# A four-layer graph network: stores of x and of the turned rows moved between node phases, a bias moved behind the shares, one phase fused, and gathers released by counts

## What is computed

```python
h = jnp.maximum(_layernorm(x, axis=-1), 0.0)
x = x + _L0_gnn_ref(h, ...)   # attention with one head: out = segment_sum(h[src] * alpha) + bias
h = jnp.maximum(_layernorm(x, axis=-1), 0.0)
x = x + _L1_gnn_ref(h, ...)   # four heads, softmax over all edges, then:
#   heads = agg + x[None]; hn = layernorm(heads) * gamma + beta; hs = hn * sigmoid(hn)
#   (hs + (x @ Wr.T + br)) @ Wo.T + bo
h = jnp.maximum(_layernorm(x, axis=-1), 0.0)
x = x + _L2_gnn_ref(h, edge_attr_128, ...)   # filters from edge features, then an MLP on the sum
h = jnp.maximum(_layernorm(x, axis=-1), 0.0)
x = x + _L3_gnn_ref(h, ...)   # h + segment_sum(h[src]), then relu(@ W1 + b1) @ W2 + b2
```

## Time and profile before

| | |
|---|---|
| time, three runs | 4364.09 us median (4363.95 to 4365.29) |
| the profiled execution | 4362.5 us, span 4360.7 us |
| PE busy | 3646.0 us (84%) |
| POOL busy | 2881.8 us (66%) |
| DVE busy | 2136.9 us (49%) |
| ACT busy | 1362.1 us (31%) |
| DMA | 364.29 MB, mean 84 GB/s |

### The profile page before, as it was taken

How to read it: one execution, slowest core, us unless ns; L and a number is a source line. 1 busy time by engine, 2 the same in 40 slices (tenths; PEclk the granted TensorE clock), 3 DMA queues, 4 the chain that set the end, 5 groups by cost and what they waited for, 6 DMA issues and landing times. The chain is left out here.

```text
span 4360.7 us, 76651 instructions
## 1 busy us (share of the span) xinstructions
PE 3646.0 (84%) x20596; PEld 3028.2 (69%) x20597; DVE 2136.9 (49%) x6551; ACT 1362.1 (31%) x1910; POOL 2881.8 (66%) x2980
## 2 busy tenths in 40 slices
PE   3649999777668999999996958888888865999997
PEld 1649999766637888888886846656555643777775
DVE  4874444333455555555554844444444446444442
ACT  2000000000041111111112847666666655444441
POOL 4877777777526777777751047777777764777772
PEclk7555555555575555555556978777777775999998
DMA  4532222222263333333322043333333333111112
GB/s 121 197 116 54 53 53 53 53 53 53 63 208 106 79 80 79 79 78 78 79 68 84 21 127 113 100 104 104 104 99 105 104 82 85 50 50 51 50 51 52
DMA packets 258518, 364.29 MB, mean 84 GB/s; under 512 B 53070, under 2 KB 179461, under 8 KB 258309
## 3 DMA queue, kind: packets, MB, share of 16 engines
q0 software_dynamic: 90624, 185.78, 16.5%
q1 hardware_dynamic: 167689, 176.37, 13.4%
HBM read 319.53 MB, written 42.41 MB: 83 GB/s over the span
## 5 line engine op out<-in xcount | busy, mean ns | idle before, releaser
L839 POOL DMA_INDIRECT m_rows<-table,e_idx x832 | 794.2, 955 | 255.8 <-issue 228.6
L839 POOL DMA_INDIRECT m_more<-table,e_idx x480 | 453.7, 945 | 145.6 <-issue 118.5
L1218 PE MATMUL e_agg<-e_weights,m_ones 128*128 128x32 f32 x1568 | 481.8, 401 | 0.0
L839 POOL DMA_INDIRECT m_hT<-table,e_idx x416 | 394.1, 947 | 125.7 <-issue 107.6
L1218 PEld LDWEIGHTS e_agg<-e_weights,m_ones 128*128 128x128 f32 x1568 | 428.5, 333 | 0.0
L839 POOL DMA_INDIRECT e_rows<-table,e_idx x352 | 342.0, 971 | 105.7 <-issue 103.9
L1217 PE MATMUL e_agg<-e_weights,m_more 128*128 128x16 f32 x1152 | 339.8, 375 | 78.3 <-issue 66.3
L1653 PE MATMUL e_z<-e_edge,e_w 128*128 128x512 f32 x392 | 262.8, 806 | 167.2 <-DVEq L1734 152.2
L805 POOL DMA_INDIRECT m_rows<-table,e_idx x320 | 307.9, 962 | 116.0 <-issue 82.3
L1217 PEld LDWEIGHTS e_agg<-e_weights,m_more 128*128 128x128 f32 x1152 | 311.5, 330 | 104.2 <-issue 104.2
L1542 PE MATMUL e_out<-e_counts,e_nodes 128*128 128x256 bf16 x2964 | 383.6, 280 | 0.0
(11 more groups left out here) (315 smaller groups left out, 7057.3 us busy)
## 6 DMA issues: line engine op xcount, KB each, us to landing
e_edge<-edge_T SPq DMA_DIRECT2D x98, 512.0 KB
lu_place<-lo_dram SPq DMA_DIRECT2D x49, 512.0 KB, 3.8
e_key<-key_dram SPq DMA_DIRECT2D x98, 256.0 KB
m_rows<-table,e_idx POOLq DMA_INDIRECT x1152, 2.5
key_dram<-key_out SPq DMA_DIRECT2D x13, 1024.0 KB, 4.7
table<-m_rows SPq DMA_DIRECT2D x39, 256.0 KB, 2.6
e_rows<-table,e_idx POOLq DMA_INDIRECT x528, 2.6
m_more<-table,e_idx POOLq DMA_INDIRECT x480, 2.5
```

The costliest lines, as they stand in the source:

```text
L839: pool.indirect_dma_start(rows[:, t, :], None, table, bass.IndirectOffsetOnAxis(ap=idx[:, t:t + 1], axis=0)).then_inc(landed[t * len(lande ...
L1218: ins = pe.matmul(to[:, 1:3, cols], m.ones[:], both[:, t, :, :], start=False, stop=(t == C - 1))
```

## The change

It does six things.

1. `attention_output` and `softmax_output` store x themselves, slab by slab, once the slab is complete (`keep_x`); the two norm phases no longer do, and only wait at their end for a semaphore `x_kept` that is handed in.
2. The turned rows are stored by `key_phase`, in four DMAs behind the two weight loads, and not by "n1_".
3. In `attention_output` GpSimd waits for the shares (`chain` at `STEPS + 1`) before it adds the bias.
4. `factor_phase` is gone. Its work is in `softmax_output`: ScalarE's exponentials at the start; the small matmuls in four parts among the products of groups 0 and 1 and the set-up; the inverse and the first part's factors ahead of group 0, the other three parts' between its measurement and its scale. The shift row lies in the first four partitions of `m.x`, which is allocated ahead of the softmax edge pass, so x is loaded only after all the small matmuls.
5. SP's order in `softmax_output`: the weights needed for products first on a semaphore of their own, h rows of group 0, the turned rows, h rows of group 1, x, the rest.
6. In `mixed_sum_edges` the gathers from round 2 on use `gather_behind` (L829): parts of two tiles, each behind a count of the count matrices that TensorE has built, in place of landings.

```diff
@@ norm_phase
-                if x_to is not None:
-                    sp.dma_start(x_to.rearrange("(n p) d -> p n d", p=P), m.x[:]).then_inc(x_kept, 16)
                 if table is not None:
                     for g in range(NG):
                         wait_rows(sp, g)
                         sp.dma_start(rows_of(g), h[g % 4]).then_inc(stored[g % 4], 16)
-                        if hT_to is not None:
-                            sp.wait_ge(t_free, g + 1)
-                            sp.dma_start(hT_to[:, g * GN:(g + 1) * GN], m.hT[:, g * GN:(g + 1) * GN]).then_inc(hT_kept, 16)
...
+                if x_kept is not None:
+                    sp.wait_ge(x_kept, 16 * len(slabs(k)))
@@ mixed_sum_edges
-                            gather_paced(pool, slots[r], idx[at.b][:, j * C:(j + 1) * C], s.gathered[r], table, at.half, s.idx_seen, ahead)
+                            steps_of = ((10, 12, 13), (16, 17, 18), (21, 23, 24))[j]
+                            gather_behind(pool, slots[r], idx[at.b][:, j * C:(j + 1) * C], s.gathered[r], table, s.idx_seen,
+                                          [(counted, at.n * L + (t + 3 - 2 * L)) for t in steps_of])
@@ attention_output
                 load_x(sp, k, m, k.dram["x_in"], x_loaded)
+                for n, (first, last) in enumerate(slabs(k)):
+                    sp.wait_ge(half_done, G4 * last)
+                    keep_x(sp, k, m, k.dram["x_dram"], n, x_kept)
...
                 pool.wait_ge(loaded, 48)
+                pool.wait_ge(chain, STEPS + 1)
                 add_bias(pool, k, m, bias, x_loaded, biased)
@@ key_phase
                 sp.dma_start(wk[:], k.dram["Wk"]).then_inc(loaded, 16)
+                for first, last in slabs(k):
+                    cols = slice(first * GN, last * GN)
+                    sp.dma_start(k.dram["hT_dram"][:, cols], m.hT[:, cols]).then_inc(hT_kept, 16)
@@ softmax_output
+                sp.dma_start(wq, k.dram["WqT"]).then_inc(wq_loaded, 16)
                 for t, d in parts:
                     sp.dma_start(t, d).then_inc(loaded, 16)
-                load_x(sp, k, m, k.dram["x_dram"], x_loaded)
                 for g in range(NG):
                     if g == 1:
+                        for n in range(PARTS):
+                            cols = slice(edges[n] * P, edges[n + 1] * P)
+                            sp.dma_start(m.hT[:, cols], k.dram["hT_dram"][:, cols]).then_inc(hT_loaded, 16)
                         sp.wait_ge(setup_ps, 1)
+                    if g == 2:
+                        sp.wait_ge(cols_ready, PARTS)
+                        load_x(sp, k, m, k.dram["x_dram"], x_loaded)
                     if g >= 2:
                         sp.wait_ge(h_rows_free, g - 1)
...
+                    for n, (first, last) in enumerate(slabs(k)):
+                        if last == g - 2:
+                            sp.wait_ge(y_taken, last)
+                            keep_x(sp, k, m, k.dram["x_dram"], n, x_kept)
...
+                pe.matmul(den_ps, m.ones[:], den[:], start=True, stop=True).then_inc(den_ready, 1)
+                columns(0)
+                pe.wait_ge(wq_loaded, 16)
                 products(0)
+                set_up()
+                columns(1)
                 products(1)
+                columns(2)
+                columns(3)
...
-                group(0)
+                def rest():
+                    for n in range(1, PARTS):
+                        factors(n)
+                group(0, rest)
+                v.wait_ge(setup_ps, 1)
+                v.tensor_copy(wro[:], y_ps[0][:, 0:P]).then_inc(setup, 1)
+                v.tensor_tensor(bo[:], bo[:], y_ps[0][:, P:2 * P], ALU.add).then_inc(setup, 1)
```

More of the change, by code:

```diff
@@ L210, in load_x, with keep_x @@
         sp.dma_start(m.x[:, cols, :], x_from.rearrange("(n p) d -> p n d", p=P)[:, cols, :]).then_inc(x_loaded[n], 16)
+def keep_x(sp, k, m, x_to, n, x_kept):
+    first, last = slabs(k)[n]
+    cols = slice(first * G4, last * G4)
+    sp.dma_start(x_to.rearrange("(n p) d -> p n d", p=P)[:, cols, :], m.x[:, cols, :]).then_inc(x_kept, 16)
 def add_bias(pool, k, m, bias, x_loaded, biased):
@@ L2276, in _ @@
                         clear_by_scalar(act, m, acc[:, h, g * GN:(g + 1) * GN]).then_inc(cleared, 1)
[L2279 to L2302, removed]
-                    for b in range(edges[n], edges[n + 1]):
-                        ins = pe.matmul(f_ps[:, b * HEADS:(b + 1) * HEADS], shift_row[:, b * P:(b + 1) * P],
-                                        m.ident[0:HEADS, 0:HEADS], start=True, stop=True)
-                ins.then_inc(cols_ready, 1)
-            @block.scalar
-            def _(act):
-                act.wait_ge(top_ready, 1)
-                for n in range(PARTS):
-                    row = shift_row[:, edges[n] * P:edges[n + 1] * P]
-                    act.activation(row, row, ACT.Exp, bias=negative[:]).then_inc(row_ready, 1)
-            @block.vector
-            def _(v):
-                v.tensor_scalar(negative[:], top[:], -1.0, None, ALU.mult).then_inc(top_ready, 1)
-                v.wait_ge(den_ready, 1)
-                v.reciprocal(inverse[:], den_ps[:, 0:HEADS]).then_inc(chain, 1)
-                v.wait_ge(chain, 1)
-                v.wait_ge(cols_ready, 1)
-                v.tensor_tensor(factor[:], f_ps[:, 0:k.NB * HEADS].rearrange("p (b h) -> p b h", h=HEADS),
-                                inverse[:].unsqueeze(1).to_broadcast([P, k.NB, HEADS]), ALU.mult).then_inc(factor_ready, 1)
-                v.wait_ge(factor_ready, 1)
@@ L2327, in softmax_output @@
-def softmax_output(nc, k, m, acc, factor):
+def softmax_output(nc, k, m, acc, shift_row, top, den, factor, x_kept):
     F = HEADS * P
@@ L2332, in softmax_output @@
     STATS = 9
+    PARTS = 4
+    edges = [k.NB * n // PARTS for n in range(PARTS + 1)]
     with ExitStack() as ctx:
@@ L2367, in _ @@
                                  ).then_inc(h_rows_loaded[g % 2], 16)
+                    for n, (first, last) in enumerate(slabs(k)):
+                        if last == g - 2:
+                            sp.wait_ge(y_taken, last)
+                            keep_x(sp, k, m, k.dram["x_dram"], n, x_kept)
+                for n, (first, last) in enumerate(slabs(k)):
+                    if last > NG - 3:
+                        sp.wait_ge(y_taken, last)
+                        keep_x(sp, k, m, k.dram["x_dram"], n, x_kept)
                 sp.wait_ge(loaded, 16 * len(parts))
+                sp.wait_ge(wq_loaded, 16)
+                sp.wait_ge(hT_loaded, 16 * PARTS)
                 for b in range(2):
@@ L2378, in _ @@
             def _(act):
+                act.wait_ge(top_ready, 1)
+                for n in range(PARTS):
+                    row = shift_row[:, edges[n] * P:edges[n + 1] * P]
+                    act.activation(row, row, ACT.Exp, bias=negative[:]).then_inc(row_ready, 1)
                 act.wait_ge(loaded, 16 * len(parts))
@@ L2456, in _, with factors @@
             def _(v):
+                v.tensor_scalar(negative[:], top[:], -1.0, None, ALU.mult).then_inc(top_ready, 1)
+                v.wait_ge(den_ready, 1)
+                v.reciprocal(inverse[:], den_ps).then_inc(inverse_ready, 1)
+                v.wait_ge(inverse_ready, 1)
                 v.wait_ge(loaded, 16 * len(parts))
                 v.tensor_copy(br_rep, over(br[:], [P, HEADS, P])).then_inc(setup, 1)
[L2459 to L2461 removed]
+                def factors(n):
+                    v.wait_ge(cols_ready, PARTS if n else 1)
+                    blocks = slice(edges[n], edges[n + 1])
+                    v.tensor_tensor(factor[:, blocks, :], f_of(n).rearrange("p (b h) -> p b h", h=HEADS)[:, blocks, :],
+                                    inverse[:].unsqueeze(1).to_broadcast([P, edges[n + 1] - edges[n], HEADS]), ALU.mult).then_inc(factor_ready, 1)
+                    v.wait_ge(factor_ready, n + 1)
+                factors(0)
                 def join(g, b):
```

68 lines of the change are left out of this document (40 added, 28 removed).

## The result

| | before | after |
|---|---|---|
| median of 4 runs | 4364.7 us (4363.95 to 4366.35) | 4314.8 us (4312.84 to 4320.33) |
| profiled execution, span | 4362.5, 4360.7 | 4312.96, 4311.2 |
| PE / POOL / DVE / ACT busy, us | 3646.0 / 2881.8 / 2136.9 / 1362.1 | 3632.9 / 2880.6 / 2142.4 / 1362.6 |

The ratio is 0.9889 (95%: 0.9875 to 0.9903): 49.9 us faster, where 36.0 were forecast. The forecast time, 4328, was 13 us too long, and the result lies at the lower edge of the range (4314 to 4343). TensorE is busy 13 us less, 7 of them at the factor columns (22.3 us before, 15.1 now, in part at the upper clock); the other engines are as busy as before, so most of the time came out of waits.

The account below looks back on a forecast made before the run. Edge passes keep an engine near its limit; node phases between them are priced by their last waits. 3.3 + 16.4 - 1.0 + 16.0 - 6.3 + 2.6 + 5.0 = 36.0 us off 4364.1 gave 4328 us, range 4314 to 4343.

Parts of the forecast that it names:

- the rival of the upper clock: Softmax output: factor columns run at the upper clock and the bias stalls nothing; 4312 us, chance 0.13.
- Step 1: Attention's output phase: bias behind the shares, shares 6.2 us sooner, 2.9 given back; net gain 3.3 us, bounds 1.5 and 6.2.
- Step 2: First norm phase: x and the turned rows stored elsewhere; gain 16.4 us, bounds 13.3 and 17.
- Step 3: Key phase: taking over the turned rows delays the key stores by 1.0 us, bounds 0 and 10.0.
- Step 4: Factor phase fused into softmax output, columns priced at the lower clock; gain 16.0 us, bounds 13 and 28.
- Step 5: Softmax output: GpSimd's bias falls over group 1's statistics and slows them; loss 6.3 us, bounds 0 and 8.4.
- Steps 6 and 7: Second norm phase loses its output-buffer wait, 2.6 us; last pass's gathers released by counts lose landing waits, 5.0 us.
- The first rival: Softmax output: columns at the upper clock, bias stalling nothing; 4312 us, chance 0.13.
- The slower rival: Softmax output: TensorE stays at the lower clock, 81 us more less the 36 gained; 4409 us, chance 0.03.

Follow-up runs that it names:

- the second measurement: The changed kernel once more, unedited, beside the kernel before on the same chip: 4319.3 us, 47.2 us faster, ratio 0.9890.
- u_bias: Changed kernel without GpSimd's wait for the shares before the bias in attention's output phase: 4322.4 us, that phase 60.6 us against 54.0.
- c_first: Changed kernel with all four quarters of the factor columns ahead of the first group's products: 4328.5 us, ratio 0.9903 to the kernel before.
- b_spaced: Changed kernel with the softmax output phase's bias additions released one by one, each by a group's finished scaling: 4318.9 us, ratio 0.9886 to the kernel before.
- g_early: Changed kernel with the last pass's gathers released two count matrices sooner: 4314.6 us, that pass 657.1 us.
- best2: Changed kernel with softmax output's bias additions released one by one and the third group's h rows loaded ahead of x: 4307.8 us, ratio 0.9877.

## Why the prediction was right, and where it was short

*Direction and place.* Every step had the forecast sign, and the three that carried the sum (2, 4 and 5) happened where they were said to. The forecast gain was 11 us too small when compared to the 47.2 of the second measurement, and 14 compared to the first. That the result still lies inside the range, by 0.8 us, is owed to the lower bound, which the rival of the upper clock and some play for a shifted edge pass had set.

*Step 1 (3.3, bound 6.2): mis-sized.* The shares came 6.5 us sooner, as worked out (6.2). The give-back failed: "three more of them (those before at 1192.4, 1195.0 and 1197.6) fall under GpSimd: 3 x 0.94 = 2.9 back". The three additions fell there, but cost 0.13, 0.47 and 0.48 more, 1.1, and the phase lost half a microsecond by it. u_bias puts the step at 6.6. The price of an operation beside GpSimd was taken from one place; GpSimd's own additions gave way here, 18.66 us for 16.90.

*Step 2 (16.4).* 17.7 at the lower clock, 19.0 to 19.5 in the three traces in which the clock rose. The phase taken as the model ends behind a clearing of semaphores and a barrier that this one doesn't have, 24.4 against 23.1.

*Step 3 (-1.0).* -2.0 to -3.5. TensorE's 104 matmuls take 46.3 us with and without the turned rows in the queue (46.37 and 46.29); they start 0.5 later, and the last key stores end later behind them, 10.3 us from TensorE's end to the next phase for 8.8. So the key stores were pushed back as said, by 1 to 2.5 us more.

*Step 4 (16.0): the largest miss.* Measured 24.1, or 21.0 where the last half of the columns takes 9 us. The step that failed is "The trace has these columns at 0.50 only, so I stay by that row". They cost 0.219 us a record at 0.50, and 0.118 at 1.00; 7.3 of the 8 us are that, the rest the set-up, 1.9 for 2.6. The row was true of columns behind columns, as c_first shows, and the change put them behind products, where a part of them runs at the upper clock before it falls. The first rival had this right (0.13) and was wrong in its other half, that the bias stalls nothing; its 4312 came about by other sums.

*Step 5 (-6.3).* 6.0 measured between groups 1 and 2. Right in size by two errors against each other: the two scalings stalled too (2.2 us more than alone), and the first and the last of the operations were stretched only to 0.56 and 0.58. That b_spaced removes it and h rows take over is the clause "landing about 2366), but VectorE gets there about 2369": the 3 us of slack are gone once the bias is.

*Steps 6 and 7 (2.6 and 5.0).* 2.0 to 3.1, and 4 to 5. GpSimd's rate was the bound that was named, and g_early shows the floor.

*The slower rival* needed the lower clock to stay through the phase. It rose during the first group's products in every trace, though it fell again behind them: in best2 it stood at 0.50 from 2321 to 2337.

## What to carry to other kernels

A phase closed by barriers is priced by its own last wait: move its transfers to where the queues are idle, and count the bytes where they arrive. A block of GpSimd additions over VectorE's small operations cost about a microsecond for each here (1.18 to 1.31 us for 0.16 or 0.17); release it one by one into slots where VectorE reads PSUM. After a wait is removed, read what was late by less than it, since that is the next one.

## What the runs showed of the hardware

The clock that TensorE is granted differs between executions of the same instructions. In ten traces with the same order of columns and products, the last 52 column records took 6.35 to 7.00 us in five and 8.73 to 9.30 in five. The first group's products, in which the clock rises, tell them apart: 5.20 to 5.90 us in the first five, 6.06 to 6.62 in the others, so a later rise goes with an earlier fall. What decides it no run shows. The first norm phase took 21.3 to 21.8 us in the three traces where the clock rose to 1.00 in it, and 23.1 in the eight where it didn't. So three microseconds of one phase and 1.5 of another can't be put down to an edit from a single trace.
